# Routing each pair of batches inside the attention loop of a two-layer Perceiver with a mixture of experts

## The reference, cut to what matters

```
x = x + xattn(layernorm(x), ctx) ; x = x + attn(layernorm(x)) ; x = x + ffn(layernorm(x))       # layer 0
x = x + xattn16(layernorm(x), ctx) ; x = x + attn16(layernorm(x)) ; x = x + moe(layernorm(x))   # layer 1

def moe(x):                                      # xf: 2048 tokens x 256, E = 8 experts, two for each token
    logits = xf @ router_w.T
    probs = jax.nn.softmax(logits, axis=-1)
    topk_p, topk_i = jax.lax.top_k(probs, TOP_K)
    topk_p = topk_p / topk_p.sum(axis=-1, keepdims=True)
    # for each expert e:
    mask = (topk_i == e).any(axis=-1)
    mean_w = (topk_p * sel).sum() / max(mask.sum(), 1)       # one gate for each expert, over all tokens
    out += mask * (silu(xf @ gate_w[e].T) * (xf @ up_w[e].T)) @ down_w[e].T * mean_w
```

## Time and profile before

| | |
|---|---|
| median of 3 runs | 2960.11 us (2958.29 to 2962.34) |
| the profiled execution's own time | 2965.66 us |
| its span, first to last instruction | 2963.8 us |
| PE, DVE, ACT, POOL busy | 2534.5, 1599.6, 1336.9, 897.0 us |
| one pass of the big loop (from a part of `ctx_lo`, at 1468.79, to the same one a pass later, at 1577.06) | 108.27 us |
| stage F; what DMA moves from 400 to 600 us | about 400 to 627 us; 1 GB/s or less |
| last output product, end of its addition to `x` | at 2440.18 us |
| first product of the experts | at 2534.87 us |

### The profile page before, as it was taken

How to read it: one execution, slowest core, us unless ns; L and a number is a source line. 1 busy time by engine, 2 the same in 40 slices (tenths; PEclk the granted TensorE clock), 3 DMA queues, 4 the chain that set the end, 5 groups by cost and what they waited for, 6 DMA issues and landing times.

```text
span 2963.8 us, 75287 instructions
## 1 busy us (share of the span) xinstructions
PE 2534.5 (86%) x32180; PEld 2148.2 (72%) x32180; DVE 1599.6 (54%) x2613; ACT 1336.9 (45%) x2115; POOL 897.0 (30%) x868
## 2 busy tenths in 40 slices
PE   6999833327999999999999999999999863799997
PEld 3555511127888888888888888888888642799997
DVE  3434367742555546456456455555645633577775
ACT  1212111115565565555555656556555321455654
POOL 1000023443434343343442443433334103111211
PEclk9999955559999999999999999999999865899999
DMA  8878600022111010010110111101001002566664
GB/s 338 326 311 326 248 0 0 0 83 64 35 36 35 24 46 24 24 46 24 35 35 24 36 35 35 35 24 45 26 24 35 2 26 89 172 209 207 200 212 148
DMA packets 48439, 270.05 MB, mean 91 GB/s; under 512 B 4882, under 2 KB 23443, under 8 KB 33555
## 3 DMA queue, kind: packets, MB, share of 16 engines
q1 hardware_dynamic: 40018, 255.69, 23.8%
q0 software_dynamic: 8160, 10.29, 2.3%
HBM read 247.45 MB, written 20.61 MB: 90 GB/s over the span
## 4 chain that ended last, share of the span: by engine, by line
PE 48%; issue 24%; POOL 10%; DVE 9%; ACT 4%; DMA 4%; POOLq 0%; SPq 0%; DVEq 0%; ACTq 0%
PE PS L1321 5%; PE PS L1179 4%; PE PS L1167 3%; POOL k_lo L550 3%; PE PS L1051 3%; POOL ctx_lo L558 3%; PE PS L1031 3%; DVE mpart L1677 2%; PE PS L1317 2%; PE PS L1156 2%; PE PS L1154 2%; PE PS L1155 2%; PE PS L1408 2%; PE PS L1409 2%; PE PS L1410 2%
## 5 line engine op out<-in xcount | busy, mean ns | idle before, releaser
L1677 DVE TENSOR_REDUCE mpart<-PS 128x1 f32<-128x802 f32 (+1 forms) x512 | 484.7, 986 | 358.1 <-PE PS L1167 356.9
L853 ACT ACTIVATE probs<-PS 128x1024 f32<-128x1024 f32 (+1 forms) x416 | 413.4, 1025 | 207.5 <-PE PS L1321 207.4
L558 POOL TENSOR_TENSOR ctx_lo<-ctx_raw,ctx_hi 128x801 fp32r<-128x801 f32 x128 | 223.0, 1753 | 397.2 <-ACT ctx_hi L793 388.6
L550 POOL TENSOR_TENSOR k_lo<-probs,k_hi 128x400 fp32r<-128x400 f32 (+1 forms) x256 | 248.9, 972 | 263.0 <-ACT k_hi L781 262.9
L1321 PE MATMUL PS<-qbd_hi,k_hi 64*128 64x256 f32 (+1 forms) x1664 | 313.5, 373 | 0.0
L1167 PE MATMUL PS<-k_hi,qbd_hi 128*128 128x512 f32 (+2 forms) x1024 | 265.7, 361 | 29.0 <-POOL ctx_lo L558 14.2
L1154 PE MATMUL PS<-wkv_hi,ctx_hi 128*128 128x256 f32 (+1 forms) x832 | 236.4, 284 | 0.0
L1321 PE MATMUL PS<-qbd_lo,k_hi 64*128 64x256 f32 (+1 forms) x1664 | 235.4, 279 | 0.7 <-issue 0.6
L780 ACT COPY probs<-PS 128x400 f32<-128x400 f32 (+1 forms) x256 | 126.3, 493 | 242.6 <-PE PS L1147 213.1
L1179 PE MATMUL PS<-probs,vals 128*32 128x64 f32 x13312 | 233.8, 221 | 2.0 <-issue 1.9
L1321 PE MATMUL PS<-qbd_hi,k_lo 64*128 64x256 f32 (+1 forms) x1664 | 234.9, 279 | 0.0
(11 more groups left out here) (322 smaller groups left out, 6071.3 us busy)
## 6 DMA issues: line engine op xcount, KB each, us to landing
unit_raw<-in_experts SPq DMA_DIRECT2D x46, 1536.0 KB, 7.1
ctxN<-in_ctxN SPq DMA_DIRECT2D x16, 3328.0 KB, 10.8
ctxT<-in_ctxT SPq DMA_DIRECT2D x16, 3204.0 KB, 10.5
ctx_raw<-in_ctxT SPq DMA_DIRECT2D x64, 801.0 KB, 4.5
slots_d<-pad_rows SPq DMA_DIRECT2D x2, 2990.0 KB, 18.5
xg<-slots_d SPq DMA_DIRECT2D x23, 260.0 KB, 2.8
x<-in_x SPq DMA_DIRECT2D x1, 2048.0 KB, 9.8
sum_d<-x SPq DMA_DIRECT2D x1, 2048.0 KB, 6.3
```

The costliest lines, as they stand in the source:

```text
L550: g.tensor_tensor(k_lo[:, n, a, c:c + width], k_raw[p % 2][:, 0:width], k_hi[:, n, a, c:c + width].bitcast(F32), ALU.subtract).then_inc(s. ...
L558: g.tensor_tensor(ctx_lo[:, a, cols], ctx_raw[:, cols], ctx_hi[:, a, cols].bitcast(F32), ALU.subtract).then_inc(s.ctx_lo_ready, 1)
L853: act.activation(probs[rows, t % PROBS, :], PS[rows, 1024 * (t % 2):1024 * (t % 2) + 1024], ACT.Exp).then_inc(s.pr_ready, 1)
L1677: v.tensor_reduce(mpart[:, pair, half:half + 1], PS[:, at:at + width], AX, ALU.max).then_inc(s.mx_red, 1)
```

## The change

It moves routing into the big loop. The pass that finishes a pair's self attention also normalizes its rows into one `xrow` (no longer 16 of them), transposes them and multiplies with the router at places 23 and 24 (`ROUTE_AT`); the next pass chooses the two experts (`choose_two`, DVE window 2), counts the rows that come before each token of the expert (`rank_tokens`, PE place 7, with `acc_m`, the masks summed so far) and finds its slots (`find_slots`, window 6); POOL scatters this tile with two indirect DMAs (`scatter`). So that a slot is known before all tiles are counted, each expert has a region of 2048 rows, and a ninth region stays padding. Because of that `slots_d` has 18432 rows instead of 5888, and its padding is written ahead of stage B's first load. Behind the loop only the last pair's routing is left, and a count from which the expert and the first row of each tile come (`expert_u`, `row_u`); SP reads the row from SBUF before each load of `xg`. The copy of `x` to `sum_d` moves behind the first three loads of `xg`.

```diff
+REGION = B * S
+REGIONS = EXPERTS + 1
...
+ROUTE_AT = (PLACES + 9, PLACES + 10)
+RANKS_AT = 7
...
+        xrow = sb("xrow", [P, ROW])
+        ids = sb("ids", [P, TILES, ROW - D], I32)
+        route = sb("route", [P, 136])
+        slot_i = sb("slot_i", [P, 2], I32)
+        tile_row = sb("tile_row", [P, SLOT_TILES])
...
-        slots_d = nc.dram_tensor("slots_d", (SLOT_TILES * SLOT_TILE, ROW), F32).ap()
+        slots_d = nc.dram_tensor("slots_d", (REGIONS * REGION, ROW), F32).ap()
...
+            sp.wait_ge(s.ids_ready, 4)
+            for k in range(SUBS):
+                sp.dma_start(slots_d.rearrange("(i s p) c -> s p i c", s=SUBS, p=P)[k],
+                             pad_rows[:, k, None, :].broadcast_to([P, REGIONS * REGION // SLOT_TILE, ROW])).then_inc(s.pads_in, 16)
...
-            sp.wait_ge(s.x_done, XDONE_B)
-            sp.dma_start(sum_d[0:B * S, :].rearrange("(p t) d -> p t d", p=P), x[:, :, :]).then_inc(s.sum_in, 16)
...
-                sp.dma_start(xg[i % TOKEN_BUFS][:, :, :], slots_d[i * SLOT_TILE:(i + 1) * SLOT_TILE, :].rearrange("(s p) c -> p s c", p=P))\
+                row = sp.value_load(row_u[0:1, i:i + 1], min_val=0, max_val=REGIONS * REGION - SLOT_TILE)
+                sp.dma_start(xg[i % TOKEN_BUFS][:, :, :], slots_d[bass.ds(row, SLOT_TILE), :].rearrange("(s p) c -> p s c", p=P))\
...
-            sp.wait_ge(s.experts_ready, 1)
+            sp.wait_ge(s.experts_ready, 2)
...
+                    sp.wait_ge(s.x_done, XDONE_B)
+                    sp.dma_start(sum_d[0:B * S, :].rearrange("(p t) d -> p t d", p=P), x[:, :, :]).then_inc(s.sum_in, 16)
...
+            def scatter():
+                g.wait_ge(s.slots_ready, slots.up())
+                g.tensor_tensor(carrier_g[:, 0:1], eps[:, :], eps[:, :], ALU.add)
+                for n in range(2):
+                    g.indirect_dma_start(slots_d[:, :], bass.IndirectOffsetOnAxis(ap=slot_i[:, n:n + 1], axis=0), xrow[:, :], None)\
+                     .then_inc(s.x_spread, 16)
...
                         spread_keys(q)
                     s4p.up(2)
+                if ranked:
+                    scatter()
                 if not last:
                     split_ctx(2)
                     split_ctx(3)
...
                     split_ctx(2)
                     split_ctx(3)
+                if not first:
+                    rsqrt()
+                    xnp.up()
+                if not last:
                     split_queries()
...
-            rsqrt_tiles(mv_m, rstd_m, TILES)
...
-            g.wait_ge(s.pads_in, 16 * SUBS)
-            g.wait_ge(s.slots_ready, 1)
-            for t in range(TILES):
-                for n in range(2):
-                    g.indirect_dma_start(slots_d[:, :], bass.IndirectOffsetOnAxis(ap=slot_i[:, n, t:t + 1], axis=0),
-                                         xrow[:, t, :], None).then_inc(s.x_spread, 16)
+            scatter()
+            rsqrt()
+            scatter()
...
+                if tile == PLACES + 9:
+                    copy_xnT(7)
+                if tile == PLACES + 12:
+                    act.wait_ge(s.rexp_in, T["rexp"].up())
+                    act.activation(chances, logits, ACT.Exp).then_inc(s.rexp_out, 1)
...
+            def rank_tokens():
+                pe.wait_ge(s.mask_ready, T["mask"].up())
+                pe.matmul(bank(7, EXPERTS), below[:, :], mask, start=True, stop=False)
+                pe.matmul(bank(7, EXPERTS), ones[:, :], acc_m, start=False, stop=True).then_inc(s.ranks_ps, 1)
+
+            def finish(place, ranked, queries):
+
+                if ranked and place == RANKS_AT:
+                    rank_tokens()
+                if place == ROUTE_AT[0]:
+                    if queries:
+                        pe.wait_ge(s.qB_ready, T["qB_sb"].now())
+                    pe.wait_ge(s.xn_ready, T["xn"].up())
+                    for k in range(KT):
+                        mm = pe.transpose(bank(7, P, at=k * P), xrow[:, k * P:k * P + P], ident[:, :])
+                    mm.then_inc(s.xn_ps, 1)
+                if place == ROUTE_AT[1]:
+                    pe.wait_ge(s.xnT_ready, T["xnT"].up())
+                    for k in range(KT):
+                        mm = pe.matmul(bank(7, EXPERTS), xnT[:, k, :], w["router"][:, k, :], start=k == 0, stop=k == KT - 1)
+                    mm.then_inc(s.logits_ps, 1)
...
+                    if ranked and q == 0:
+                        pe.wait_ge(s.places_ready, T["places"].up())
...
+            rank_tokens()
+            pe.wait_ge(s.acc_ready, TILES - 1)
+            pe.matmul(bank(5, EXPERTS), ones[:, :], acc_m, start=True, stop=False)
+            pe.matmul(bank(5, EXPERTS), ones[:, :], mask, start=False, stop=True).then_inc(s.rsum_ps, 1)
...
+            def choose_two():
+                def stepped(ins):
+                    ins.then_inc(s.vec_step, 1)
+                    v.wait_ge(s.vec_step, own())
+                v.wait_ge(s.rexp_out, T["rexp"].up())
+                stepped(v.tensor_reduce(largest, chances, AX, ALU.max))
+                stepped(v.scalar_tensor_tensor(hot_rank, chances, largest, rank[:, :], ALU.is_equal, ALU.mult))
+                stepped(v.tensor_reduce(first_rank, hot_rank, AX, ALU.max))
+                stepped(v.tensor_scalar(hot[:, 0, :], hot_rank, first_rank, None, ALU.is_equal))
+                stepped(v.scalar_tensor_tensor(left, hot[:, 0, :], -4.0, chances, ALU.mult, ALU.add))
+                stepped(v.tensor_reduce(second, left, AX, ALU.max))
+                stepped(v.scalar_tensor_tensor(hot_rank, left, second, rank[:, :], ALU.is_equal, ALU.mult))
+                stepped(v.tensor_reduce(second_rank, hot_rank, AX, ALU.max))
+                stepped(v.tensor_scalar(hot[:, 1, :], hot_rank, second_rank, None, ALU.is_equal))
+                v.tensor_tensor(mask, hot[:, 0, :], hot[:, 1, :], ALU.add).then_inc(s.mask_ready, 1)
+                stepped(v.tensor_tensor(both, largest, second, ALU.add))
+                v.reciprocal(both_inv, both).then_inc(s.vec_step, 1)
+                v.tensor_scalar(gates, hot[:, 0, :], largest, None, ALU.mult).then_inc(s.vec_step, 1)
+                v.wait_ge(s.vec_step, T["step"].up(2))
+                stepped(v.scalar_tensor_tensor(gates, hot[:, 1, :], second, gates, ALU.mult, ALU.add))
+                v.scalar_tensor_tensor(acc_g, gates, both_inv, acc_g, ALU.mult, ALU.add).then_inc(s.vec_step, 1)
+                T["step"].up()
+
+            def find_slots():
+                v.wait_ge(s.ranks_ps, T["ranks"].up())
+                v.tensor_tensor(place, bank(7, EXPERTS), region, ALU.add).then_inc(s.places_ready, 1)
+                v.wait_ge(s.places_ready, T["places"].up())
+                v.tensor_tensor(picked, hot, place[:, None, :].broadcast_to([P, 2, EXPERTS]), ALU.mult).then_inc(s.vec_step, 1)
+                v.wait_ge(s.vec_step, own())
+                v.tensor_reduce(slot_f, picked, AX, ALU.add).then_inc(s.vec_step, 1)
+                v.wait_ge(s.vec_step, own())
+                v.tensor_copy(slot_i[:, :], slot_f).then_inc(s.slots_ready, 1)
+            def finish(window, xi, numbers, ranked, spread):
+
+                if ranked and window == 2:
+                    choose_two()
...
+                    if ranked:
+                        find_slots()
+                        v.tensor_tensor(acc_m, acc_m, mask, ALU.add).then_inc(s.acc_ready, 1)
...
+                    v.wait_ge(s.x_done, T["x_done"].up(2))
+                    v.tensor_copy(carrier_v[:, :], eps[:, :])
+                    moments(xi)
+                if window == PLACES + 8:
+                    if spread is not None:
+                        v.wait_ge(s.x_spread, spread)
+                    v.tensor_copy(xrow[:, D:ROW].bitcast(I32), numbers)
+                    normalize(xi, xrow[:, 0:D]).then_inc(s.xn_ready, 1)
+                if window == PLACES + 10:
+                    v.wait_ge(s.logits_ps, T["logits"].up())
+                    v.tensor_reduce(logit_max, bank(7, EXPERTS), AX, ALU.max).then_inc(s.vec_step, 1)
+                    v.wait_ge(s.vec_step, own())
+                    v.tensor_scalar(logits, bank(7, EXPERTS), logit_max, None, ALU.subtract).then_inc(s.rexp_in, 1)
...
+            choose_two()
+            v.wait_ge(s.vec_step, T["step"].now())
+            v.tensor_copy(rsmall[:, 40:48], acc_g).then_inc(s.rsum_ready, 1)
+            find_slots()
+
+            v.wait_ge(s.rsum_ps, 1)
+            tiles_of, ends, counts = (spans[:, n * EXPERTS:(n + 1) * EXPERTS] for n in range(3))
+            v.tensor_scalar(counts, bank(5, EXPERTS), 1.0 / SLOT_TILE, (SLOT_TILE - 1) / (2.0 * SLOT_TILE), ALU.mult, ALU.add).then_inc(s.vec_step, 1)
+            v.tensor_scalar(rsmall[:, 16:24], bank(5, EXPERTS), 1.0, None, ALU.max).then_inc(s.vec_step, 1)
+            v.memset(past[:, 0:1, :], 1.0).then_inc(s.vec_step, 1)
+            v.wait_ge(s.vec_step, T["step"].up(3))
```

(48 more changed lines are left out.)

220 lines of the change are left out of this document (52 added, 168 removed).

## The result

The changed kernel takes 2944.9 us (median of 5 runs, 2943.21 to 2949.14), the kernel before 2958.29 us beside it (5 runs, 2957.88 to 2962.34): a ratio of 0.9949, 95% interval 0.9937 to 0.9960. It is faster, but by 13 us and not by 46, and lies 10 us above the range.

A forecast was written before the change was run, and what follows sets the result against it. PE was taken to bound the loop (105.73 of 108 us busy), an engine-to-engine chain the stretch behind it. -65.0 + 18.5 + 0.5 = -46.0, so 2960.1 - 46.0 = 2914 us; range 2899 to 2935.

The forecast's parts named there:

- Tail, -65.0: Behind the loop, from the last addition to `x` to the first expert product: shrinks from 94.7 us, 65.0 us less.
- The lower bound of 58: Smallest saving behind the loop, 58 us, if each of the 40 small steps costs 0.15 us more.
- Products in the loop, +18.5: On PE in the loop: transposes, router and rank products add 15 x 0.83 + 14 x 0.43 = 18.5 us.
- Place 23 with 0.6 us of slack: In the loop, PE's transposes need normalized rows at 1537.9, PE begins at 1538.51: slack 0.6 us, the thinnest, cost nothing.
- Rival 1: Loop pays more than the products, PE stalling at four new waits: 1 to 1.5 us a pass, 2929 to 2937; 20%.
- `choose_two`, 3.2 us in 7.63 of idle time: On DVE in the loop: choosing two experts takes 3.2 us, where DVE idled 7.63 us, at no cost.
- The scatter, slack 2.5, at nothing: On POOL in the loop: two scatter DMAs leave 2.5 us of slack before PE needs `ctx_lo`'s fourth part, costing nothing.
- rival 3: Starved scatter in the loop: POOL blocked two to three times as long, 7 us more, 2921; inside the forecast's 65%.
- rivals 3 and 4: The fourth: slower than before, scatter on POOL holding up `ctx_lo`'s fourth part, 2965 and more; 3%.
- Padding, third unit: Padding takes some 58 us, hidden under stage F; the copy to `sum_d` delays the experts' third unit, costing 0.5 us.
- The base: Starting point of the sum: profiled execution before 2965.66 us, 5.6 above the three runs' median; carried to median 2960.1.

The follow-up runs named there:

- The kernel with the first tile first: Against the kernel with the scatter moved into POOL's idle time between batches: the first tile's rows load right behind the first unit of weights; 2916.83 us.

## Why the prediction was wrong

Point by point, by its own steps:

- **Tail, -65.0.** Right: 94.7 to 27.0 us, -67.7. Slots came 9.0 us behind the addition (10.3 foreseen), the first weights 13.2 (14.7), `xg` ended last and at 24.5 (27.2), 2.5 to the first product as before. Of the 2.7 us 1.3 lie in the steps to the slots and 1.2 between the first weights and `xg`. (The lower bound of 58 was a slip, 40 steps of 0.15 make it 59.)
- **Products in the loop, +18.5.** Right: a second set of them makes a pass 1.29 longer, and in the kernel with the scatter moved a pass is 1.08 longer than before where 1.26 was counted.
- **Place 23 with 0.6 us of slack.** Right: PE's transposes of `xrow` have no wait of note in the loop, only the 3.14 us of the tile behind it. Rival 1's mechanism did not happen, though its time came nearest.
- **`choose_two`, 3.2 us in 7.63 of idle time.** The size was wrong (6.7), the price nearly right: it is hidden. What I left out: two of its operations wait for POOL. The Trainium skill ("SBUF — State Buffer", Who interferes with whom) says that VectorE's two-input operations in SBUF, and those that use two ports, share a port pair with GpSimd under an exclusive lock; the trace agrees, with 0.23 and 0.17 us alone against 1.56 and 1.81 beside `ctx_lo`.
- **The scatter, slack 2.5, at nothing.** This is the step that failed. As far as it went it held: 2.3 us for two DMAs on POOL (1607.69 to 1610.03), no held-up `ctx_lo` on PE's path, none of rival 3's 3.1 us a DMA, so rivals 3 and 4 fell. (Rival 3 was also added up wrongly: 1 us late in each of 14 passes is 14, not 7.) But I asked only who is queued behind the scatter on POOL and not what stands beside it on PE, the engine that bounds the loop. Beside it stood 64 products within 1.1 us, and 2.2 us a pass went there: 28.4 us by the run with the scatter moved, of the 31 that the forecast was off. Of the 32 scatters of before nothing could show it, they ran with PE idle. The same trace does have indirect DMAs beside PE, the experts' 46 of L664. 44 of them have the experts' products of 256 columns beside them, and PE has no idle spell of over 0.1 us there. The prediction left them out; they say nothing of small products, but show which place is harmless. I had bounded the cost of this step by durations on POOL alone; the upper bound for a new neighbour of the bounding engine was missing.
- **Padding, third unit.** Padding landed in 44.8 us (median of the two) under stage F, hidden. The copy to `sum_d` took 13.6 instead of 6.3 us, and from the first expert product on nothing is longer: 0 instead of 0.5, though this stretch lies between 428.9 and 432.4 us in the experiments, so that half a us can't be told there.
- **The base.** The sum was made against an execution 5.6 us above its median and carried over to the median. With the hold-up taken away the kernel takes 2916.5 where 2914 was predicted. That this is so near is in part luck: it is 49.9 us less from trace to trace (2963.8 to 2913.9) and 43.6 less by the medians of that comparison (2960.16 to 2916.54), the long execution of before makes most of the difference, and the 46 of the sum happens to lie between.

The last pair takes 4.9 us longer than before, and 2.0 to 4.9 in the experiments, where routing and one hold-up explain 1.3 to 3.5. The rest goes with TensorE's clock. Windows of the last pair, in the columns of the earlier trace rows, first of the changed kernel, then of the kernel with the scatter moved, which does the same work there:

```profile
2364.87:2450.56 85.69, 72.31 (x1325) 54.71 (x1323) 43.59 (x91) 30.47 (x40) 6.08 (x11) 0.83 0.02 5
2336.75:2419.54 82.79, 69.26 (x1325) 52.59 (x1323) 43.42 (x92) 30.46 (x40) 6.08 (x11) 0.88 0.02 5
```

With a mean granted clock of 0.83 instead of 0.88 PE is busy for 3.05 us more with as many products, and the pair is 2.9 longer. The kernel with the first tile first has 0.83 and 85.67 as well. Why the clock was lower in these two executions is not shown; the other 2.0 us are within what routing and the hold-up explain.

One thing stays open: by what path an indirect DMA slows the other engines. The same Trainium skill page and section say "PE and ACT never wait on anyone", which is about SBUF's ports, and here both wait, so that these ports are not the likely place. The Trainium skill's "Runtime: NRT & Kernel Launch" (Instruction fetch mechanics) says that an engine fetches its program through a DMA queue of its own and that this is mostly hidden; the trace agrees in that there is such a queue, with 238 packets and 3.90 MB. But plain DMAs with as much traffic held up nothing, and PE has the spells without a packet of that queue in sight. The scatter that begins at 1164.50 has the same three, of 0.42 us, the last ending at 1167.33, and from 1164.5 to 1168 all packets are those of the scatter's own queue:

```profile
DMA packets 96, 0.27 MB, mean 76 GB/s; under 512 B 32, under 2 KB 32, under 8 KB 96
q0 software_dynamic: 96, 0.27, 21.1%
```

## What to carry to other kernels

A step moved to an idle engine isn't free because that engine's queue has room: ask also what the bounding engine does in those microseconds, above all where it issues many short instructions. Where a trace has never shown two things side by side, give the new neighbourhood a price on both sides, and look first for a place under wide products; here one moved line was worth 28 us, more than twice the whole change. In a trace after, compare each group's busy plus idle time with the same group before: the 28.8 us at `weigh` stood in one row.

## What the runs showed of the hardware

- Beside 64 products of 64 columns that take 1.10 us alone, an indirect DMA of 128 rows from GpSimd slowed TensorE's issue: one DMA gave one idle spell of 0.43 us and cost 0.7 us, two in a row gave three, about 0.75 us apart, and cost 2.1 us (means over 13 passes).
- It did so with rows of 16 bytes as with 1040, and plain DMAs of the same size from the same queue did not.
- Beside 256 to 512-column products two of them cost nothing that can be measured, six of them 1.3 us a pass, through ACT and DVE starting late.
- Two of VectorE's operations over 8 numbers, a TENSOR_SCALAR and a SCALAR_TENSOR_TENSOR, ended only with the GpSimd operation over 801 columns beside them, after 1.56 and 1.81 us instead of 0.23 and 0.17. A TENSOR_REDUCE beside the first of them (at 1595.49) took 0.16, as it does alone.
- The last pair took 85.7 us at a mean granted clock of 0.83 and 82.8 at 0.88, with the same products.
